# The place of the sixth rope gather in the opening of an attention and feed-forward kernel

## The reference, cut to what matters

```
h = layernorm(x)
q, k, v = h @ Wq, ctx @ Wk, ctx @ Wv           # 32, 8 and 8 heads of 128
q, k = q*cos + rotate_half(q)*sin, k*cos + rotate_half(k)*sin
p = softmax(mask(q @ k.T / sqrt(128)))
x = x + (p @ v) @ Wo
y = x + layernorm(x) @ dequantised_fp4(kernel) + bias
```

## Time and profile before

| | |
|---|---|
| median of 3 runs | 1145.03 us (1144.58 to 1145.14) |
| the profiled execution's own time | 1145.21 us |
| its span | 1143.1 us, 19747 instructions |
| PE busy | 1132.4 us, 99% of the span |
| DVE, ACT, POOL busy | 813.0, 765.1, 629.0 us |
| granted clock of TensorE | 1.00 of full speed |
| chain that ended last | PE 93%, DVE 2%, POOL 2%, issue 1%, ACT 1%, DMA 1% |

### The profile page before, as it was taken

One profiled execution on the slowest core, in us unless ns is written; L12 is line 12 of the kernel. 1 busy time (PEld: TensorE's weight loads), 2 busy tenths in 40 slices (PEclk: granted clock), 3 DMA queues, 4 the chain that ended last, 5 costly groups with the idle time before them and its releaser, 6 DMA issues.

```text
span 1143.1 us, 19747 instructions
## 1 busy us (share of the span) xinstructions
PE 1132.4 (99%) x6346; PEld 975.9 (85%) x6358; DVE 813.0 (71%) x1753; ACT 765.1 (67%) x2301; POOL 629.0 (55%) x518
## 2 busy tenths in 40 slices
PE   7999999999999999999999999999999999999998
PEld 6888888888888888888888788888888888888876
DVE  8777777777777777689787766656666665666698
ACT  6866777566676766688666566676766677665663
POOL 7854655365554655579656455544655446545433
PEclk9999999999999999999999999999999999999999
DMA  8211211112111111224212221110201112020001
GB/s 260 84 28 48 74 34 51 33 43 65 34 51 33 61 38 38 93 71 140 56 52 72 83 67 56 33 52 19 84 1 37 47 38 65 11 73 21 1 4 71
DMA packets 51748, 63.47 MB, mean 56 GB/s; under 512 B 8768, under 2 KB 27584, under 8 KB 51648
## 3 DMA queue, kind: packets, MB, share of 16 engines
q1 hardware_dynamic: 50736, 59.86, 17.0%
q0 software_dynamic: 768, 2.10, 0.6%
q10 hardware_dynamic: 144, 0.26, 0.1%
HBM read 58.01 MB, written 4.19 MB: 54 GB/s over the span
## 4 chain that ended last, share of the span: by engine, by line
PE 93%; DVE 2%; POOL 2%; issue 1%; ACT 1%; DMA 1%; POOLq 0%; ACTq 0%; DVEq 0%
PE proj L510 15%; PE proj L511 15%; PE proj L512 15%; PE pS L613 9%; PE pO L667 8%; PE pO L668 8%; PE pO L669 8%; PE pV L645 3%; PE pV L646 3%; PE pT L628 2%; PE pO L677 2%; PE proj L564 1%; PE proj L558 1%; PE pO L680 1%; PE proj L524 1%
## 5 line engine op out<-in xcount | busy, mean ns | idle before, releaser
L819 ACT CAST PS<-pT 64x256 fp32r<-64x256 f32 x256 | 93.8, 366 | 294.0 <-PE pV L646 290.6
L1288 POOL TENSOR_TENSOR t<-t,SIN 128x512 f32<-128x512 f32 x124 | 159.7, 1288 | 188.5 <-ACT t L828 188.1
L510 PE MATMUL proj<-XH,QH 128*128 128x512 f32 x512 | 201.3, 393 | 0.1
L512 PE MATMUL proj<-XH,QL 128*128 128x512 f32 x512 | 199.5, 390 | 0.0
L511 PE MATMUL proj<-XL,QH 128*128 128x512 f32 x512 | 199.3, 389 | 0.0
L667 PE MATMUL pO<-OH,AH 128*128 128x512 f32 x432 | 171.4, 397 | 0.0
L668 PE MATMUL pO<-OL,AH 128*128 128x512 f32 x432 | 169.1, 391 | 0.0
L669 PE MATMUL pO<-OH,AL 128*128 128x512 f32 x432 | 168.4, 390 | 0.0
L1292 POOL TENSOR_TENSOR qT<-qT,t 128x512 f32<-128x512 f32 x124 | 159.5, 1286 | 9.7
L1031 DVE TENSOR_TENSOR qT<-proj,COS 128x512 f32<-128x512 f32 x128 | 88.4, 690 | 95.2 <-PE proj L512 56.7
L882 ACT ACTIVATE pS<-pS,tiny 128x64 f32<-128x64 f32 x512 | 143.0, 279 | 10.6 <-DVE tiny L1194 6.3
(11 more groups left out here) (197 smaller groups left out, 2566.5 us busy)
## 6 DMA issues: line engine op xcount, KB each, us to landing
QR<-wq SPq DMA_DIRECT2D x64, 256.0 KB, 2.7
OR<-wo SPq DMA_DIRECT2D x62, 256.0 KB, 3.0
CR<-ctxT SPq DMA_DIRECT2D x16, 256.0 KB, 5.7
KR<-wk SPq DMA_DIRECT2D x16, 256.0 KB
UR<-wv SPq DMA_DIRECT2D x16, 256.0 KB
acc<-x SPq DMA_DIRECT2D x15, 256.0 KB, 3.3
out<-acc SPq DMA_DIRECT2D x15, 256.0 KB, 2.0
rawx<-x SPq DMA_DIRECT2D x8, 256.0 KB, 2.9
```

Of the source, the lines that this page charges most:

```text
L510: pe.matmul(dst, lh, rh, start=k == 0, stop=False)
L512: made = pe.matmul(dst, ll, rh, start=False, stop=k == last)
L1288: pool.tensor_tensor(t[:, :], t[:, :], SIN[:, 512 * (s % 2):512 * (s % 2) + 512], ALU.mult).then_inc(g_qs, 1)
```

## The change

One call of `gather` is moved up by two places in POOL's order.

```
@@ -1308,9 +1308,9 @@
             gather(4)
             low(PLACE["q", 0, 1])
             inverse_pair(4)
+            gather(5)
             low(PLACE["q", 0, 2])
             inverse_pair(6)
-            gather(5)
             low(PLACE["q", 0, 3])
             for n in range(FIRST, END):
                 if is_last(n):
```

## The result

The changed kernel takes 1148.07 us (median of 8 runs, 1146.01 to 1149.41) and the kernel before 1144.62 us (8 runs, 1144.50 to 1145.14). The ratio is 1.0026, with a 95% interval of 1.0016 to 1.0035. The change costs some 3.4 us where I forecast 0.3. The runs also lie in two groups: six at 1147.81 to 1149.41 us, with a mean granted clock of 0.998 or 0.999, and two at 1146.01 and 1146.28 us with 1.000. The kernel before has 1.000 in its profile.

A forecast was written before the change was run, and what follows sets the result against it. PE, busy 99% of the span, was taken as the bound. Removing the gather wait (-0.70 us) and starting query 2 later (+0.95) gave +0.25 us, forecast 1145.3 us, range 1144.4 to 1145.9.

The forecast's parts named there:

- its wait: PE's pause for gather 5's rows after query 2, from 24.61 to 25.31 us; 0.70 us was the most to gain.
- The chain from the pair over the shifts, the products of query 0 and the bank of query 2: POOL's inverse deviations of tiles 6 and 7 release DVE's shifts, then query 0's products, whose end frees query 2's bank on PE.
- its slack of 0.15 us: Query 2 could have started at 21.60 but started at 21.75; any delay of DVE's shifts beyond 0.15 us delays it.
- DVE stands until about 19.02, does its 0.58 to 19.6, and the pair ends 0.58 later at 20.2: L968 waits for query 2's low weights on POOL; shifts 1.1 us late, query 2 0.95 late, net +0.25 us; chance 0.52.
- one scene at 503 us: L941 on DVE took 1.20 us, usually 571 ns, waiting for one POOL instruction; the next POOL instruction was stretched to 1.47.
- the cases by who starts first: At L968: DVE held first, +0.25 us (0.52); POOL held first, +0.55 (0.19); no hold-up, 0.18 earlier (0.20).
- my range of plus 0.55 us: Upper end 1145.9 us: 1145.03 plus 0.55 for POOL held first plus 0.3 scatter, leaving out a late gather 6.
- The rule of the Trainium skill: Two-SBUF-input VectorE and SBUF-reading GpSimd instructions share ports; the first holds them its whole length, so 0.25 or 0.55 us slower.
- The slowest rival: Gather 6, issued at 24.1 us, lands late and PE waits for it: 1146.5 to 1147.0 us; chance 0.05.

The follow-up runs named there:

- kernels with a pause: The changed kernel with POOL waiting for L968's end ahead of (1145.61 us) or behind (1145.31 us) the inverse deviations of tiles 6 and 7.
- extra_in_place_of_gather: The changed kernel with gather 5 issued only ahead of gather 6 and an unused POOL subtraction of 128x512 in its early place; 1146.75 us, ratio 1.0016.

## Why the prediction was wrong

The frame was right. PE does its list without a stop, so what happens at query 2 goes straight to the end. The gather started at 16.7 us on the old scale, landed in time, and its wait disappeared with 0.70 us. The chain from the pair over the shifts, the products of query 0 and the bank of query 2 was the right one, and its slack of 0.15 us was as thin as worked out. Gather 6 made nobody wait.

**The step that failed** is "DVE stands until about 19.02, does its 0.58 to 19.6, and the pair ends 0.58 later at 20.2". The low weights did start first, by 0.07 us. But DVE then stood until 21.4 (21.0 on the old scale), through three instructions of POOL. I had taken one scene at 503 us, where DVE had its turn behind the first POOL instruction, as the rule for the turn. That scene is typical of its own kind: over the whole kernel before, no instruction of L941, L947 or L972 lasts more than 1.67 us. But each of these reads one large tensor, and L968 reads two. The kernels with a pause show that this turn exists and has just the price I gave it (0.23 measured, 0.25 worked out). The changed kernel doesn't get it. I had also sorted the cases by who starts first, where the real question was how long the holder goes on. The low weights of query 3 moved up by the change as well: before, gather 5 stood between the pair and them. I counted what the gather's new place delays and not what its old place had kept apart. With a stop between the pair and the low weights of query 3, and the gather as early, L968 took 1.78 us; that a gather there would have done the same is argued, not shown.

The shifts were priced by the pair's end alone. They also stand behind L968 in DVE's own list, and that was the wait that ended last: the pair was done at 20.14, the shifts began at 21.88.

**The missing term** is the clock. I priced PE's wait by its length. At 1.9 us it costs 1.59 us more in the profiled execution, through products at 1.2 GHz. The six runs of eight with a mean clock under 1.000 are those that paid it, to judge by their times. Behind waits of 0.65 and 0.86 us, as in the kernels with a pause, and behind the 1.45 us for the late gather in extra_in_place_of_gather, PE ran on at a granted clock of 1.00. So a late query 2 has a step in its price, and my range of plus 0.55 us ended below it. The step alone doesn't explain the miss: the two runs without it, at 1146.01 and 1146.28 us, are above the range too.

The rule of the Trainium skill that I weighed (page "SBUF — State Buffer", section "SBUF: two separate sides") gave the right direction: the first to start holds the ports and the other is blocked. A two-SBUF-input instruction on DVE that comes second is now in a trace, at 3.73 us. But one instruction's length, which the rule gives, is less than what the runs show: the hold went on over three and four instructions.

The slowest rival, gather 6 as the wait in place of gather 5, came nearest to the measured time (1147.0 us), but by another road: PE waited for no gather in the changed kernel.

**Left open:** what decides at the end of a POOL instruction whether DVE gets in. It is shown that behind a gather the hold lasts to the row's end, or to the pair where that stands last, and that with a subtraction in the gather's place it ends behind the low weights of query 2. Why that is so no run tells, nor whether the gather as such decides or how long the row has been going when L968 comes. It also stays open why a wait of 1.9 us costs the clock in six runs of eight in one kernel and in three or five of ten in others; only profiled executions show the wait itself.

## What to carry to other kernels

Before an instruction is moved on POOL, look at what it kept apart: the end of a row of arithmetic is where L968, with its two SBUF inputs, got through at the latest in every kernel here. Put what another engine waits for at the head of such a row. Price a DVE instruction of this kind that meets the row by one instruction at best (1.74 to 1.79 us here) and by the row's full length at worst (3.73 and 4.95 us). Add to a new wait of PE the chance that its clock falls behind it: at 1.9 us that happened in 3 of 10 to 6 of 8 runs here, behind the waits of 0.65, 0.86 and 1.45 us it did not, and sixteen transposes of the identity took that part away.

## What the runs showed that I had not expected

- A DVE subtraction of 128x512 with both inputs in SBUF took 0.68, 1.78, 3.04, 3.73 or 4.95 us, by what POOL did beside it.
- Over the same three POOL instructions it took 3.73 us behind a gather and 1.75 us behind a subtraction.
- POOL's own instructions keep their usual length through the long hold (1.29, 0.73 and 1.29 us); only where DVE gets in is the next one stretched, the pair from 0.73 to about 1.2 us.
- One wait of PE of 1.88 us was followed by 3.6 us at a granted clock of 0.54. The two runs of the same kernel with a mean clock of 1.000 were 1.5 to 3.4 us faster than the six others.
